# Attention over a sorted edge list on one core: VectorE's order inside one pair of blocks in the gather phase

## The reference

```
q = (embeds[rows] @ qW).reshape(e, HEADS, dh)
k = (embeds[cols] @ kW).reshape(e, HEADS, dh)
v = (embeds[cols] @ vW).reshape(e, HEADS, dh)
scores = jnp.clip(jnp.einsum('ehd,ehd->eh', q, k), -10.0, 10.0)
exp_s = jnp.exp(scores)
norms = jax.ops.segment_sum(exp_s, rows, num_segments=nvar)[rows]
w = exp_s / (norms + 1e-08)
res = jax.ops.segment_sum(w[:, :, None] * v, rows, num_segments=nvar).reshape(nvar, d)
...
x = _layernorm(x + (embeds + res), axis=-1)
```

## Time and profile before

| what | value |
|---|---|
| median of 3 runs | 1902.27 us (1899.31 to 1902.39) |
| the profiled execution | 1900.21 us |
| its span, first to last instruction | 1898.4 us |
| mean granted TensorE clock | 0.918 |
| PE, DVE busy | 83%, 80% of the span |
| ACT, POOL busy | 61%, 56% of the span |

### The profile page before, as it was taken

The page is one execution under the profiler, slowest core; times in us unless marked ns, Lnnn a source line. Parts: engine busy times, 40 slices in busy tenths (PEclk is TensorE's granted clock), DMA queues, the critical chain, the costliest instruction groups (busy, mean ns, idle before and its releaser), DMA issues.

```text
span 1898.4 us, 60193 instructions
## 1 busy us (share of the span) xinstructions
PE 1569.5 (83%) x19628; PEld 1479.1 (78%) x19629; DVE 1518.0 (80%) x3658; ACT 1155.5 (61%) x2254; POOL 1058.3 (56%) x969
## 2 busy tenths in 40 slices
PE   4856888788788778888748999999999999999990
PEld 3735777777777777777748999999999999999990
DVE  6878778777777777777717888888888888888887
ACT  3343545444544445444437888888888888888871
POOL 5233777777777777777763444444444444444440
PEclk9567889999989999889978999999999999999995
DMA  5464888888888888888879777777777777776741
GB/s 162 169 236 148 313 313 314 305 306 301 303 317 309 301 297 312 302 311 305 299 260 284 225 222 223 226 218 222 223 221 225 220 222 226 218 228 217 227 141 51
DMA packets 203224, 470.79 MB, mean 248 GB/s; under 512 B 42592, under 2 KB 75616, under 8 KB 196730
## 3 DMA queue, kind: packets, MB, share of 16 engines
q1 hardware_dynamic: 156156, 306.11, 52.1%
q0 software_dynamic: 47040, 164.33, 22.3%
HBM read 281.07 MB, written 202.00 MB: 254 GB/s over the span
## 4 chain that ended last, share of the span: by engine, by line
PE 51%; DMA 18%; DVE 11%; issue 10%; POOL 5%; ACT 2%; SPq 1%; DVEq 1%; ACTq 0%; POOLq 0%
DMA sorted_rows<-work 14%; PE meta L1135 13%; PE sum_bank L1135 11%; PE two_a L1153 6%; PE two_b L1153 6%; POOL sorted_rows L596 5%; PE two_a L1058 3%; PE two_b L1058 3%; PE one_c L1143 3%; PE one_d L1143 3%; DMA work<-sorted_local 2%; DVE work L1412 1%; DVE work L1419 1%; PE one_d L1099 1%; ACT work L847 1%
## 5 line engine op out<-in xcount | busy, mean ns | idle before, releaser
L596 POOL DMA_INDIRECT sorted_rows<-work x588 | 640.0, 1088 | 208.9 <-issue 188.2
L653 POOL TENSOR_TENSOR work<-work 128x576 f32<-128x576 f32 x312 | 362.9, 1163 | 499.5 <-ACT work L889 499.5
L898 ACT ACTIVATE work<-work 128x768 f32<-128x768 bf16 x312 | 402.1, 1289 | 0.0
L1058 PE MATMUL two_a<-work 128*128 128x192 bf16 x2352 | 249.7, 261 | 116.7 <-DVE work L1380 109.5
L1058 PEld LDWEIGHTS two_a<-work 128*128 128x128 f16 x2352 | 201.9, 103 | 127.5 <-DVE work L1380 68.3
L1135 PE MATMUL meta<-work 128*128 128x100 f32 x1872 | 243.1, 280 | 43.1 <-issue 37.2
L1135 PEld LDWEIGHTS meta<-work 128*128 128x128 f32 x1872 | 221.7, 192 | 61.2 <-issue 61.2
L1058 PE MATMUL two_b<-work 128*128 128x192 bf16 x2352 | 254.1, 264 | 0.0
L1523 DVE TENSOR_REDUCE work<-work 128x24 f32<-128x576 f32 x312 | 235.0, 753 | 10.8
L1135 PE MATMUL sum_bank<-work 128*128 128x100 f32 x1872 | 241.6, 279 | 0.2 <-DVE acc L1497 0.2
L1058 PEld LDWEIGHTS two_b<-work 128*128 128x128 f16 x2352 | 219.6, 106 | 3.4
(11 more groups left out here) (237 smaller groups left out, 2793.7 us busy)
## 6 DMA issues: line engine op xcount, KB each, us to landing
work<-sorted_rows SPq DMA_DIRECT2D x624, 294.0 KB, 3.0
work<-sorted_local SPq DMA_DIRECT2D x49, 1152.0 KB
work<-kv_table SPq DMA_DIRECT2D x196, 144.0 KB
sorted_rows<-pad_rows SPq DMA_DIRECT2D x49, 294.0 KB, 4.3
sorted_rows<-work POOLq DMA_INDIRECT x588
kv_table<-work SPq DMA_DIRECT2D x12, 576.0 KB, 3.4
work<-in_x SPq DMA_DIRECT2D x12, 192.0 KB, 3.8
out<-acc SPq DMA_DIRECT2D x4, 576.0 KB
```

The lines of the kernel that those rows point to most:

```text
L596: pool.indirect_dma_start(out=rows_dram, out_offset=bass.IndirectOffsetOnAxis(ap=place_now[:, u, b:b + 1], axis=0), in_=payload[:, u, b * ...
L653: pool.tensor_tensor(now[:, :, 0:D].rearrange("p c (h f) -> p c h f", h=HEADS), blk[:, k, :, :, D:2 * D].rearrange("p m c (h f) -> p (m c) ...
L898: act.activation(hot_f[:, k % HOTF], hot[:, k % HOTS].rearrange("p n c -> p c n"), ACT.Copy).then_inc(hotf_made[k % PSEM], 1)
L1058: mm = pe.matmul(to, picked[:, u % 2, k * P:(k + 1) * P], window[:, u, :, n, :], start=(n == 0), stop=(n == 2))
```

## The change

In each slot of the gather DVE now makes both additions with the clipping between them, and then the next pair's one-hot. Nothing is added or removed, and the other engines' programs keep their order.

```diff
                 for s in range(SBI):
                     add(s, 0)
+                    if at := lagged(s, 4, j, drain):
+                        k, back = at
+                        pair_done(dve, score_made, k, back, at_j)
+                        dve.tensor_scalar(clipped[:, k].rearrange("p c h -> p (c h)"), score[:, k], -CLIP, CLIP,
+                                          ALU.max, ALU.min).then_inc(clip_made[k % PSEM], 1)
+                    add(s, 1)
                     if at := lagged(s, 1, j, drain):
                         k, back = at
                         pair_done(dve, tag_made, k, back, at_j)
...
                         dve.tensor_tensor(hot[:, k % HOTS], tags[:, k, :].unsqueeze(1).to_broadcast([P, P, CH]),
                                           node1_row[:], ALU.is_equal).then_inc(hot_made[k % PSEM], 1)
-                    add(s, 1)
                     if s == SBI - 1 and not drain:
                         tiles_of(dve, tiles, plus(dve, j, 1), LA)
-                    if at := lagged(s, 4, j, drain):
-                        k, back = at
-                        pair_done(dve, score_made, k, back, at_j)
-                        dve.tensor_scalar(clipped[:, k].rearrange("p c h -> p (c h)"), score[:, k], -CLIP, CLIP,
-                                          ALU.max, ALU.min).then_inc(clip_made[k % PSEM], 1)
```

## The result

The changed kernel takes 1878.55 us (median of 4 runs, 1875.93 to 1882.03) against 1900.94 before (4 runs): a ratio of 0.9882, with a 95% interval of 0.9869 to 0.9896. It is 1.2% faster. The forecast was 1888, faster, in a range of 1877 to 1912. Four kernels further down have a name ending in _b: in their first series every kernel was 16 to 19% slower, the kernel before too (2242 us), so their second series is compared.

A forecast was written before the change was run, and what follows sets the result against it. PE, held by a loop through DVE of 5.18 us per two slots against its own 4.98. A round of 7 x 2.49 + 3.64 + 0.24 = 21.31 instead of 21.66, 14 us gained in all, gave 1888 us, range 1877 to 1912.

The forecast's parts named there:

- The loop of 5.18 us over two slots: In the gather, PE's sums wait on a loop through DVE, 0.20 us longer than PE's own work; it falls to 4.94.
- The main case: Gather's short PE waits go, DVE's slot becomes 2.53 us; round 21.31 instead of 21.66, gain 14 us, time 1888.
- all of it arrives: Gather with the one-hot's wait steps free and DVE's slot 2.50 us: 20 to 22 us less, about 1881; chance 0.2.
- The two additions stood 0.40 apart: On DVE, the second addition would start 0.40 us behind the first instead of 0.64, as in the drain.
- The load in slot 7: DVE's load now follows the one-hot; the product comes at A + 1.62 or A + 1.92, hidden behind PE's own load.
- A: The start of the first addition in a DVE slot, from which the prediction counts times in us.
- the price of the one-hot's waits: On DVE, delay of the one-hot past A + 0.57 by its extra wait steps: 0 to 0.055 us, taken as 0.03.
- a drift of 0.04 us: DVE's slot of 2.53 us exceeds PE's by 0.04, building up over six slots to 0.24 per round.
- The rival in which POOL takes the port: In the gather, POOL's product starts before DVE's one-hot and blocks it: 287 us in every slot, about 2190; chance 0.18.
- the lead of 0.10: The one-hot on DVE would start at A + 0.57, 0.10 us ahead of POOL's product at A + 0.67.
- the 0.42 us behind POOL's end: A one-hot on DVE blocked by POOL's product would end 0.42 us after that product.
- DVE as the new bound: DVE slots of 2.58 to 2.62 us replace PE's wait: within 4 us of 1902; no measurable change 0.16, longer DVE 0.06.

The follow-up runs named there:

- clip_only: Kernel before, with the clipping moved behind the first addition and the one-hot still between the two additions; 1917.31 us, ratio 1.0075.
- sums_last: Kernel before, DVE's order unchanged, PE's sums moved to the end of its slot, behind the q matmuls; 1863.10 us, ratio 0.9806.
- sums_last_after: Changed kernel, with PE's sums moved to the end of its slot; 1869.98 us, ratio 0.9833 to the kernel before.
- one_wait: Changed kernel, with one wait on the one-hot instead of three; 1879.98 us, ratio 0.9892 to the kernel before.
- clip_first: Kernel before, with DVE's order made clipping, addition, addition, one-hot; 2168.46 us, ratio 1.1403.
- both_loads: Changed kernel, PE's tile-number load moved under slot 0's sums and DVE's load between slot 7's product and reduction; 1853.54 us, ratio 0.9752 to the kernel before.
- add_only: Kernel before, with both additions in a row, then the one-hot, the clipping still last; 1915.34 us, ratio 1.0074.

## Why the prediction was right

The direction, the place and the mechanism held. The loop of 5.18 us over two slots with PE's own 4.98 inside it was read rightly: clip_only lengthened it and lost, sums_last gave PE slack and won, and sums_last_after left the change nothing to do. The main case itself did not come: its own range was 1881 to 1896, and with 1878.55 us and a round of 21.18 the result lies nearest to "all of it arrives" (about 1881, a round of 21.07 to 21.13), which had 0.2 of the 0.60. It is inside the stated range by 1.5 us, which is less than the spread of the runs, so that the number held at its low end is in part luck. The two additions stood 0.40 apart, as the drain had shown. The load in slot 7 was hidden, with the product at A + 1.82, between the two values given.

The step that was mis-sized is the price of the one-hot's waits. I took 0.03 us, between 0 and 0.055, and a drift of 0.04 us in each of six slots. Measured against A + 0.57, the one-hot is 0.01 late in plain slots and 0.04 and 0.03 late in the two with a register instruction; in one_wait, without the two extra waits, it is still 0.01 late in plain slots, so there they cost nothing, and 0.03 in slot 1. Their 0.05 us each, seen in slot 7, stays hidden. A slot of DVE is 2.50 and PE's round 21.18, not 21.31. That is 5 of the 9 us by which 1888 was too slow; one more is the median of the kernel before, 1900.94 with a fourth run, and the rest I can't place. The lower bound of that price was the better value; an operation behind an addition starts 0.17 us after it anyway.

The rival in which POOL takes the port was given 0.18. It did not come, but its two numbers did: the lead of 0.10 was 0.09, and the 0.42 us behind POOL's end was 0.42 in clip_first; its 287 us in every slot were 268 there. DVE as the new bound, the other rival, came in its mildest form: in the changed kernel the slots of 2.50 are DVE's, since DVE waits for q only once a round. The sum of that rival was too low at its upper end: a slot of 2.62 or 2.63 is 0.13 or 0.14 above PE's 2.49, six times that less the 0.59 won makes 7 to 9 us slower in 37 rounds, not within 4 or about 5.

## What to carry to other kernels

Where a busy engine still waits a little, follow the loop through its buffers until it closes, and compare its length with the engine's own work. What a new order can gain ends at the next bound, here DVE's own slot of 2.50 us, 0.01 above PE's 2.49. Two dependent short operations left a hole of 0.15 us here; the clipping, which fits in it, made the reordering pay, and the large one-hot belongs outside the loop. Before such a move, look at what the moved operation will newly run beside: an order of three operations with POOL's product 0.28 us ahead cost 14%.

## What the runs showed of the hardware

The product on POOL and the one-hot on DVE, both with two SBUF inputs, block each other in both directions: a one-hot of 0.55 us lasted 1.30 behind POOL's product, and a product of 1.16 us lasted 1.48 behind the one-hot. A load of 16 numbers into registers left DVE idle for 0.80 us behind an addition of 0.25, 0.70 behind the one-hot of 0.55 and 0.47 behind a product of 0.75. Against the same two operations without a load that is 0.88, 0.77 and 0.44 us more from start to start; it is less behind longer work, which suggests that part of the load runs beside that work. one_wait bears this out for the one-hot: two waits fewer ahead of the one-hot left its start where it was and brought the product behind the load 0.10 us forward, so the load does not begin only at the one-hot's end. The same pair of runs gives 0.05 us of the sequencer for a wait that is already met. On PE the same load left 0.96 to 0.99 us of idle time behind 18 short matmuls. Behind the long sums of slot 0 the slot with the load took 2.94 us in both_loads (1403.43 to 1406.37) against 3.64, and even it was held by DVE's addition at its end. PE's boundary of 4.11 us in add_only stays open.
